# Quantised weights summed in place, their masks added in the next block

## The reference

```python
def _L0_xattn_ref(query, value, wq, wk, wv, wo):      # 32 query heads, 8 key heads, D = 128
    q = (query @ wq).reshape(b, tq, HQ, D)
    k = jnp.repeat((key @ wk).reshape(b, tk, HKV, D), REP, axis=2)
    v = jnp.repeat((key @ wv).reshape(b, tk, HKV, D), REP, axis=2)
    probs = jax.nn.softmax(jnp.einsum('bqhd,bkhd->bhqk', q * (1.0 / jnp.sqrt(D)), k), axis=-1)
    return jnp.einsum('bhqk,bkhd->bqhd', probs, v).reshape(b, tq, HQ * D) @ wo
...
    def nf4_quant_dequant(w):                          # w1, w2, w3 of layer 2, each 1376 x 512
        flat = w.reshape(-1, 64)
        absmax = jnp.max(jnp.abs(flat), axis=1, keepdims=True)
        normalized = flat / jnp.where(absmax == 0, 1.0, absmax)
        idx = jnp.searchsorted((NF4_CODE[:-1] + NF4_CODE[1:]) * 0.5, normalized)
        return (NF4_CODE[idx] * absmax).reshape(shape)
...
x = x + jnp.tanh(g_xattn[0]) * _L0_xattn_ref(_layernorm(x), ctx, ...)
x = x + jnp.tanh(g_ffn[0]) * _L0_ffn_ref(_layernorm(x), ...)   # 4-bit weights: nibbles, zero, scale
```

## Time and profile before

| | us |
|---|---|
| median of 3 runs (lowest, highest) | 1568.92 (1562.45, 1570.29) |
| the profiled execution's own time | 1567.22 |
| its span | 1565.5 |
| busy in the span: TensorE, VectorE, ScalarE, GpSimd | 1383.2, 1120.4, 677.5, 331.8 |
| the first stage's seven blocks with weights, up to VectorE's first addition of block 7 | 413.86 |

### The profile page before, as it was taken

How to read it: one execution, slowest core, us unless ns; L and a number is a source line. 1 busy time by engine, 2 the same in 40 slices (tenths; PEclk the granted TensorE clock), 3 DMA queues, 4 the chain that set the end, 5 groups by cost and what they waited for, 6 DMA issues and landing times.

```text
span 1565.5 us, 18720 instructions
## 1 busy us (share of the span) xinstructions
PE 1383.2 (88%) x6532; PEld 990.5 (63%) x6532; DVE 1120.4 (72%) x2045; ACT 677.5 (43%) x1403; POOL 331.8 (21%) x380
## 2 busy tenths in 40 slices
PE   6999999989997979987999997999999999999204
PEld 5665566556585648664788875677777777777102
DVE  4778877887887996946555555666665666667998
ACT  3777766776623443421222223444444444343104
POOL 1111111111155020221211111122122122122530
PEclk9999999999998999976999998999999999999557
DMA  5588888788820001412221310011011011000001
GB/s 210 154 203 192 180 206 202 176 182 195 191 93 1 1 27 60 85 33 68 48 68 40 112 54 14 28 41 68 27 41 68 27 41 68 1 1 1 0 0 55
DMA packets 37831, 127.76 MB, mean 82 GB/s; under 512 B 4928, under 2 KB 10944, under 8 KB 31536
## 3 DMA queue, kind: packets, MB, share of 16 engines
q1 hardware_dynamic: 26224, 83.38, 16.1%
q0 software_dynamic: 11520, 43.26, 14.5%
HBM read 72.63 MB, written 10.75 MB: 53 GB/s over the span
## 4 chain that ended last, share of the span: by engine, by line
PE 62%; DVE 20%; ACT 6%; DMA 5%; DVEq 4%; issue 2%; POOL 1%; POOLq 0%; SPq 0%
PE PS L150 11%; PE PS L152 11%; PE PS L151 11%; DMA AR<-AR 4%; DVE AR L670 4%; PE PS L913 4%; PE PS L949 4%; ACT s_sb L603 2%; DVE AR L676 2%; DVE AR L2498 2%; PE PS L935 2%; PE PS L531 2%; DVE AR L2487 2%; DVE AR L2494 2%; PE PS L506 2%
## 5 line engine op out<-in xcount | busy, mean ns | idle before, releaser
L434 POOL DMA_DIRECT2D AR<-AR x76 | 69.3, 1024 | 370.1 <-DVE AR L689 188.9
L531 PE MATMUL PS<-R,PT 128*128 128x512 f32 x256 | 122.2, 622 | 1.9 <-DVE X L710 1.8
L151 PE MATMUL PS<-R16r 128*128 128x512 f32 (+1 forms) x328 | 122.6, 374 | 0.0
L152 PE MATMUL PS<-R16r 128*128 128x512 f32 (+1 forms) x312 | 119.7, 384 | 0.0
L506 PE MATMUL PS<-R,HT 128*128 128x256 f32 x512 | 116.2, 380 | 2.3 <-ACT R L592 2.3
L506 PEld LDWEIGHTS PS<-R,HT 128*128 128x128 f32 x512 | 94.8, 190 | 14.5 <-ACT R L592 2.8
L603 ACT ACTIVATE s_sb<-PS,sm 128x64 f32<-128x64 f32 x256 | 77.9, 336 | 52.6 <-DVE sm L695 51.9
L1058 ACT COPY AR<-PS 128x512 f32<-128x512 f32 x64 | 37.5, 585 | 144.5 <-PE PS L152 144.1
L150 PE MATMUL PS<-HTr,R16r 128*128 128x512 f32 (+1 forms) x240 | 89.8, 374 | 3.0 <-DVE R16r L188 1.6
L150 PE MATMUL PS<-R16r,HTr 128*128 128x512 f32 (+1 forms) x224 | 90.2, 403 | 0.0
L531 PEld LDWEIGHTS PS<-R,PT 128*128 128x128 f32 x256 | 50.2, 200 | 60.2 <-issue 56.8
(11 more groups left out here) (311 smaller groups left out, 3590.0 us busy)
## 6 DMA issues: line engine op xcount, KB each, us to landing
AR<-AR POOLq DMA_DIRECT2D x76, 528.0 KB, 6.8
OR<-in_wo SPq DMA_DIRECT2D x12, 1024.0 KB, 4.9
dequantised<-AR SPq DMA_DIRECT2D x8, 1056.0 KB, 5.4
WR<-in_w0q SPq DMA_DIRECT2D x8, 1024.0 KB, 4.9
AR<-in_w3q SPq DMA_DIRECT2D x8, 1024.0 KB, 5.0
WR<-dequantised SPq DMA_DIRECT2D x22, 256.0 KB, 2.8
AR<-in_nf SPq DMA_DIRECT2D x4, 1056.0 KB, 6.7
nf_in<-in_nf SPq DMA_DIRECT2D x4, 1056.0 KB, 6.8
```

Of the source, the lines that this page charges most:

```text
L151: nc.tensor.matmul(out, ah, bl, start=False, stop=False)
L152: return nc.tensor.matmul(out, al, bh, start=False, stop=last_)
L434: nc.gpsimd.dma_start(nf_below(g)[:, part], what[:, part], accum_op=ALU.add, max_dma_last_dim=4 * N_NF // 2).then_inc(added, 16)
L531: i = nc.tensor.matmul(bank(5 + tt), PT[:, at:at + P], vo[:, pr, b, :], start=pr == 0, stop=pr == 1)
```

## The change

1. `up(7)` of a block writes its result into `nf_below(g)` instead of `nf_above`. All five masks, mask 0 too, go to other buffers and are added by DMA, and there is no `join`. A block has five pairs of accumulating transfers as before.
2. The masks of block g are made in block g + 1 (`masks`): two in turn 0, two in turn 1, one in turn 2. GpSimd starts the first addition after `up(7)` and mask 0.
3. `up(0)` waits for no transfer. `up(7)` of block g waits for all additions of block g - 1; mask k (k from 2) waits for the addition of mask k - 2, mask 1 for the store of the block before.
4. The steps up, the maxima and the reciprocals stand in other turns, and `far` 7, 8 and 9 earlier.
5. `load_nf` follows the last mask (turn 2, not the end of the block), `load_q` stands ahead of it, the store and the loads behind it wait for the fifth addition of a block, which now is in the next block; the load of `KR_W` waits for the last sum instead of the last addition.
6. The four norm pairs of layer 0's second norm stand between the last additions on GpSimd.

```diff
-            return nf_ring(g + 1 if k % 2 else g + 2)
+            return nf_ring(g + 1 + (k + (g == LATE)) % 2)
...
             for g in range(NG):
+                if g + 2 < NG:
+                    load_q(g + 2)
                 if g:
                     if g + 1 < NG:
                         load_nf(g + 1)
+                    if g == LATE:
+                        sp.wait_ge(A0["nf_summed"], LATE * NSUM)
+                        sp.dma_start(KR_W, l1kr_d).then_inc(A1["kr_in"], 16)
                     nf_store(sp, g - 1)
                 if g + 2 < NG:
-                    load_q(g + 2)
                     load_o(g + 2)
...
         def accumulate(pool, g, k):
-            pool.wait_ge(A0["nf_mask"], g * NDOWN + max(k + 1, 2))
-            nf_add(pool, g, k, nf_mask(g, k), "nf_left")
-            nf_add(pool, g, k, nf_mask(g, k), "nf_right")
+            if g == LATE:
+                n = k
+                pool.wait_ge(A0["nf_mask"], g * NDOWN + max(k + 1, 2))
+            else:
+                n = k + 1
+                if k == 0:
+                    pool.wait_ge(A0["nf_summed"], (g + 1) * NSUM)
+                pool.wait_ge(A0["nf_mask"], g * NDOWN + n)
+            nf_add(pool, g, n, nf_mask(g, k), "nf_left")
+            nf_add(pool, g, n, nf_mask(g, k), "nf_right")
...
             for g in range(LATE):
-                for k in range(1, NDOWN):
+                for k in range(NDOWN):
                     accumulate(pool, g, k)
-                join(pool, g)
+                    if g == LATE - 1 and k >= 2:
+                        pool_norm_pair(pool, 1, k - 2)
+            pool_norm_pair(pool, 1, PAIRS - 1)
...
-                    far(act, g, 2 * b + 1)
-                    far(act, g, 2 * b + 2)
+                    far(act, g, 2 * b + (2 if b == 3 else 1))
+                    far(act, g, 2 * b + (3 if b == 3 else 2))
...
-                if g < LATE and b == B - 1:
-                    far(act, g, NFAR)
+                if g < LATE and b == 2:
+                    far(act, g, 7)
...
             if k == 0:
-                if g:
-                    dve.wait_ge(A0["nf_left"], nf_added(g - 1, NDOWN))
-                    dve.wait_ge(A0["nf_right"], nf_added(g - 1, NDOWN))
                 nc.vector.tensor_scalar(nf_above, nf_in(g), bound, rise, ALU.is_gt, ALU.mult)\
                     .then_inc(A0["nf_summed"], 1)
             else:
+                out = nf_above
+                if k == NUP - 1 and g < LATE:
+                    out = nf_below(g)
+                    if g:
+                        dve.wait_ge(A0["nf_left"], nf_added(g - 1, NDOWN))
+                        dve.wait_ge(A0["nf_right"], nf_added(g - 1, NDOWN))
...
+            elif k == 1:
+                if g:
+                    dve.wait_ge(A0["nf_stored"], 16 * g)
+            elif k or g:
+                n = nf_added(g, k - 1) if k else nf_added(g - 1, NDOWN - 1)
                 dve.wait_ge(A0["nf_left"], n)
                 dve.wait_ge(A0["nf_right"], n)
...
+        def masks(dve, g, b):
+            for k in ((0, 1), (2, 3), (4,), ())[b]:
+                down(dve, g, k)
+            if b == 2:
+                dve.drain().then_inc(A0["nf_used"], 1)
...
                 norm(u + 1)
+                if g:
+                    masks(dve, g - 1, b)
...
             for u in range(LATE * B, NU0):
...
                 if u + 1 < NU0:
                     norm(u + 1)
+                masks(dve, LATE - 1, b)
...
-            pool_norm(pool, 1)
```

More of the change, by code:

```diff
@@ L383, in nf_store @@
             sp.wait_ge(A0["nf_right"], nf_added(g, NDOWN))
-            if g == LATE - 1:
-                sp.dma_start(KR_W, l1kr_d).then_inc(A1["kr_in"], 16)
             n = NBU * QB
@@ L427, in sp_x0, with nf_add @@
                     sp_f0(sp)
-        def nf_add(pool, g, k, what, side):
+        def nf_add(pool, g, n, what, side):
             added = A0[side]
             part = slice(0, N_NF // 2) if side == "nf_left" else slice(N_NF // 2, N_NF)
-            if g or k > 1:
-                pool.wait_ge(added, nf_added(g, k - 1))
+            if g or n > 1:
+                pool.wait_ge(added, nf_added(g, n - 1))
             nc.gpsimd.dma_start(nf_below(g)[:, part], what[:, part], accum_op=ALU.add,
@@ L679, in down @@
         def down(dve, g, k):
[L680 to L685, removed]
+            if g == LATE:
+                if k == 0:
+                    dve.drain()
+                if k == 2:
+                    dve.wait_ge(A0["nf_stored"], 16 * g)
+                else:
+                    n = nf_added(g, k - 2) if k > 2 else nf_added(g - 1, NDOWN - k)
+                    dve.wait_ge(A0["nf_left"], n)
+                    dve.wait_ge(A0["nf_right"], n)
+            elif k == 1:
+                if g:
+                    dve.wait_ge(A0["nf_stored"], 16 * g)
+            elif k or g:
+                n = nf_added(g, k - 1) if k else nf_added(g - 1, NDOWN - 1)
                 dve.wait_ge(A0["nf_left"], n)
@@ L688, in down @@
             bound, fall = DOWN[k]
-            nc.vector.tensor_scalar(nf_mask(g, k) if k else nf_below(g), nf_in(g), bound, fall, ALU.is_le, ALU.mult)\
-                .then_inc(A0["nf_mask"], 1)
+            nc.vector.tensor_scalar(nf_mask(g, k) if k or g < LATE else nf_below(g), nf_in(g), bound, fall,
+                                    ALU.is_le, ALU.mult).then_inc(A0["nf_mask"], 1)
+        def masks(dve, g, b):
[3 more added lines that the diff above has]
+                dve.drain().then_inc(A0["nf_used"], 1)
         def dve_x0(dve):
@@ L723, in dve_x0 @@
                 norm(u + 1)
+                if g:
+                    masks(dve, g - 1, b)
                 if b == 0:
-                    down(dve, g, 1)
-                    down(dve, g, 0)
-                elif b == 1:
-                    up(dve, g, 1)
-                    down(dve, g, 2)
-                elif b == 2:
-                    down(dve, g, 3)
-                    up(dve, g, 3)
-                else:
-                    up(dve, g, 5)
-                if more and b == 2:
-                    nf_reciprocal(dve, g + 1)
+                    up(dve, g, 0)
+                else:
+                    up(dve, g, 2 * b - 1 + b // 3)
+                if more and b == 3:
+                    nf_max(dve, g + 1)
                 shift(u + 2)
                 if b == 0:
-                    up(dve, g, 0)
                     lowest(dve, g, 0)
@@ L742, in dve_x0 @@
                 elif b == 1:
-                    if more:
-                        nf_max(dve, g + 1)
                     up(dve, g, 2)
@@ L747, in dve_x0 @@
                     up(dve, g, 4)
-                    down(dve, g, 4)
+                    up(dve, g, 5)
                 else:
-                    up(dve, g, 6)
+                    if more:
+                        nf_reciprocal(dve, g + 1)
                     up(dve, g, 7)
-                    dve.drain().then_inc(A0["nf_used"], 1)
-                if more and b == 3:
-                    nf_normalise(dve, g + 1)
+                    if more:
+                        nf_normalise(dve, g + 1)
             for u in range(LATE * B, NU0):
```

2 lines of the change are left out of this document (1 added, 1 removed).

## The result

The change made the kernel slower. Its median is 1588.72 us (1587.47 to 1591.59, 4 runs) against 1568.74 us (1562.45 to 1570.29, 4 runs) for the kernel before on the same chip, a ratio of 1.0138 with a 95% interval of 1.0107 to 1.0169: 20.0 us by the medians, 21.6 by the ratio. The forecast was 1555 us, faster, with a range up to 1572; both the sign and the range are wrong. The profiled execution has a span of 1584.5 us, 19 above.

What follows compares the result with a forecast made beforehand. It took TensorE as nearly full, VectorE close behind, with waits costing 6.4 us a block. Block 0 -2, blocks 1 to 5 -17, block 6 -4 and block 7 +11 gave -12: 1567.2 to 1555 us, range 1543 to 1572.

Steps and rivals of the forecast that it cites:

- The wait at `up(7)` for ScalarE goes too: VectorE's wait for ScalarE's far 9 at `up(7)` would vanish, saving 3 us a block.
- block 7's +11: Block 7, with short turns, would take 11 us more from masks, mask 3's wait and loads; between +6 and +15.
- -17 (blocks 1 to 5): Blocks 1 to 5 would each take 49.8 us instead of 53.2, 17 us less in all.
- -4 (block 6): Block 6 would take 45.8 us instead of 49.8, losing two waits and gaining mask 3's.
- L: Time of one pair of accumulating transfers, bounded by 5.9 to 11.6 us and taken as 7.3.
- quick: Rival: pairs take at most 5.5 us, no wait at mask 3, blocks of 47.0, 1535 us; chance 0.08.
- slow chain: Rival: a pair takes 9 us, mask 3 waits 7.1, blocks stay at 53.2, 1579 us; chance 0.15.
- VectorE: 46.1 + 3.7 = 49.8: Middle blocks' period in us: VectorE's own 46.1 plus a 3.7 wait at mask 3; TensorE's figure was 50.7.
- the norm pairs on GpSimd ... have slack: GpSimd's norm pairs in block 7 would come one to two additions late at worst, with slack.
- ScalarE's copy ... lands at about 48 ... 0 to 3, within the bound: Block 7: layer 1's weight load would land about 48 us after the block's first addition, costing 0 to 3 us.
- D: A block's first addition on VectorE, from which the prediction counts times within the block.
- It does nothing on TensorE: Rival: `up(0)`'s wait was already hidden, block 7's +11 stands alone, 1578 us; counted within the slow case's 0.15.

Runs made afterwards that it cites:

- experiment 1: The changed kernel with far 7 made in turn 2 ahead of the first half of the exponentials, not behind both: 1573.44 us, ratio 1.0042 to the kernel before.
- experiment 4: The kernel before with far 9 made in turn 3 ahead of the first half of the exponentials, not behind both: 1552.39 us, ratio 0.9891.
- Experiment 2: The changed kernel with layer 1's weight load issued ahead of the store of block 6 instead of behind it: 1583.43 us, ratio 1.0096 to the kernel before.
- experiment 3: The changed kernel with a buffer of its own for mask 3 of block 6: 1591.24 us, ratio 1.0151 to the kernel before.
- experiment 5: The changed kernel with three of the four norm pairs behind the last addition on GpSimd: 1587.26 us, ratio 1.0120 to the kernel before.
- experiment 11: The changed kernel with far 7 early, layer 1's weight load ahead of block 6's store and three norm pairs behind the last addition: 1566.23 us, ratio 1.0005.
- experiment 6: The changed kernel without the masks of block 6 and their additions (work left out): 1568.67 us, ratio 1.0009 to the kernel before.
- experiment 9: The kernel before with SP's load of the next block's quantised weights behind the store, far 9 unmoved: 1547.10 us, ratio 0.9868.
- after: The changed kernel, against the kernel before: 1588.72 us, ratio 1.0138.
- experiment 8: The changed kernel with far 7 early, layer 1's weight load ahead of block 6's store and an own buffer for its mask 3: 1573.35 us, ratio 1.0042.
- experiment 10: The changed kernel with far 7 early and layer 1's weight load ahead of block 6's store, no own mask buffer: 1566.32 us, ratio 0.9994.
- experiment 7: The kernel before with far 9 early and SP's load of the next quantised weights behind the store: 1534.74 us, ratio 0.9785.

## Why the prediction was wrong

**The step that failed first** is "The wait at `up(7)` for ScalarE goes too: far 9 now stands ahead of turn 3's pieces and exponentials". True of far 9, but the change pulled `up(5)` from turn 3 into turn 2, and its far 7 stands behind turn 2's exponentials. The same 3.00 us came back one turn earlier. So the term "3 us a block" for ScalarE's arrays was nothing. I had followed the step that was moved forward and not the one that took its place. Priced by experiments 1 and 4: 15 to 17 us. The second step that failed is block 7's +11, below. Term by term the prediction had -2 (block 0), -17 (blocks 1 to 5), -4 (block 6) and +11 (block 7), -12 in all; the traces have -0.4, +1.2, -2.6 and +24.6, 22.8 more at the next attention's first copy and 19 at the end.

**The additions.** L was put at 7.3. In block 3 the first pair is issued 3.98 us after the block's first addition (209.93), and mask 3's wait for the second ends at 17.24, so L = (17.24 - 3.98 - 0.2) / 2 = 6.5. Mask 3 is reached at 14.85, forecast 14.9. The wait is 2.4 instead of 3.7, so this term was a little too dear; but a second wait of 1.6 at mask 4, which I had only in a rival, makes 4.0 again. Mask 4 waits for the third pair. Its right half, issued at 223.38, has landed only by 233.7, after 10.3 us, beside the 1 MB load of query weights that SP issues at 222.54; the change had given this load a new place. Experiment 1's trace has the same (issued at 216.27 and 216.75, the mask at 226.27), but no run moved that load. By the fixed part and the rate in the Trainium skill, "DMA: Bandwidth & Descriptors", section on the anatomy of one DMA, a pair would take 4.5 us as an estimate; the trace has 6.5 in block 3. In block 7 it is 7.7, the mean of two unlike pairs: the right half of the first, beside the scales' loads and 1 MB for `KR_W` issued at 412.13, has landed by 427.08, 10.3 us after the pair's issue, and that of the second takes 5.2 (427.08 to 432.30). So neither quick nor slow chain came about.

**The block period** "VectorE: 46.1 + 3.7 = 49.8" would have been 46.1 + 2.4 + 1.6 = 50.1 without the far 7 wait; experiment 1, without it, has 50.7, TensorE's figure in the prediction. Of the -17 us for blocks 1 to 5 some 12 would have been there.

**Block 6 and block 0** gave 2.6 and 0.4 us, together 3 where I had 6.

**Block 7** was put at +11, between +6 and +15; it is +24.6. From the block's first addition to ScalarE's first copy of the next attention's probabilities it took 502.76 - 413.86 = 88.9 us before and takes 525.51 - 412.02 = 113.5. Of this 11.2 lie ahead of turn 2's addition: forecast 22 to 25 us after the first, measured 24.4, right, and right in its terms too (masks 4.8 forecast and 4.9 measured, mask 3's wait 4.7 and 4.1, loads 1.5 and 2.2). The rest comes behind it. "TensorE's chain behind them is full up to the next norm, so nothing absorbs this" was right, but the chain also grew. Turns 2 and 3, from addition to addition, take 8.4 and 9.3 us for 7.0 and 7.7: 3.0 more, with the outputs behind the 9.3 us stall at 6.67 us for 3.67 and a granted clock of 0.89 over 412 to 460, where it was 1.00 (2.4 GHz throughout) over 414 to 450 before. Then "the norm pairs on GpSimd ... have slack" and "ScalarE's copy ... lands at about 48 ... 0 to 3, within the bound" both failed. The additions are 9 us apart with a norm pair between them, so the fifth lands at D + 46.6 and not at 41; the load leaves at D + 47.3, and ScalarE's copy comes at D + 55.3 and not at 48. The transposes behind it (L264, 474.24) stand at D + 62.2, before (454.61) at D + 40.8: 21.4 more, so that 21.4 - 11.2 - 3.0 = 7.2 are left for the load and what hangs on it. Experiment 2 bears this out: the stretch is 7.3 us shorter there, and 5 to 7 us of it reach the end. The other 6 or so are those 3.0 and 3.1 more behind 474.24, where the first matmuls again run slower (1.09 us for 0.60 at L264); over the whole stretch the granted clock is 0.88, where it was 0.96. How they split between the slower clock and the norm pairs was not measured by itself: experiments 3, 5 and 11 show only that removing one wait brings up the next, and experiment 6 that without block 6's masks 20.2 of the 24.6 us go. The 4.4 that stay are not theirs; VectorE's wait of 2.5 us for the scales is among what is left.

**The rivals.** None had this outcome, and all stayed below it. "Slow chain", 1579, and "It does nothing on TensorE", 1578, came nearest, both with no gain in the blocks and a costly block 7. But the slow chain's reason didn't come about: it wants a pair of 9 us and 7.1 at mask 3, and block 3 has 6.5 and 2.39. The other's is refuted: experiments 4 and 9 show each removed wait to be worth 16 to 20 us. The waits did count; at `up(0)` the time came back at the masks, and at `up(7)` it came back at `up(5)`.

**What was aimed at.** The join's wait could be had for nothing. The prediction named the load beside the joining pair ("ran with a full load started at the same time") and used it only to price L. Experiment 9 shows that it was the cause: with the load behind the store the pair takes 7.4 us for 11.6, and is hidden.

## What to carry to other kernels

When a step is moved forward, check what it now reads and what stands in its place: a wait tied to "the step ahead of the exponentials" moves with the slot, not with the step. Before a transfer is removed, ask why it is long; here its length was the load issued beside it, and swapping two lines on SP was worth 20 us where a rewrite was worth nothing. Work deferred into the next block has to go somewhere after the last one: price that tail on every engine and queue, the loads behind the deferred store and small work on the issuing engine too.

## What the runs showed of the hardware

A pair of accumulating transfers of 528 KB a half takes 7.4 us from issue to landing with no load issued beside it (experiment 9); back to back, pairs follow each other every 6.5 us (block 3 of after). Beside a load it takes longer: 10.3 us beside the scales and 1 MB issued 4.6 us ahead of it (block 7 of after), 11.6 beside 1.1 MB issued with it (before), and 14.1 (412.98 to 427.11) beside 1.3 MB issued 2.4 us after its first half (experiment 8).

GpSimd's first computation behind its own accumulating transfers comes late. Its norm pair is two instructions with a drain between. Behind an issue the second began 8.35 us after the last issue in after (432.49 to 440.84), 8.4 in experiment 10, and 14.3 in experiment 8, where the transfer itself was drawn out by a load and landed at 427.1, 2.7 us ahead of it. So a drawn-out transfer draws out the delay. But a transfer under way isn't needed for it. Experiment 6 has no addition in block 7; its store of block 5 is issued at 408.46, so all additions had landed by then, and still its first norm pair stands 5.07 us between the two instructions:

```profile
430.73 0.22 POOL L233 TENSOR_SCALAR veps<-mv 128x2 f32<-128x2 f32 x1 [31.57 <-DVE mv L175]
436.01 0.72 POOL L235 TENSOR_TENSOR rstd<-veps,half 128x2 f32<-128x2 f32 x1 [5.07 <-issue]
```

The kernel before has 3.48 us there (427.12), with its last addition landed by 421.76, when the store leaves. The norm pairs that follow next without an issue between (459.94 in after, 430.65 in before) have 0.2 us or less there. What GpSimd waits for in these cases, and whether it is the drain, no run shows.

TensorE's clock can fall to its lower level behind a stall: in after's block 7 it is 0.89 over 412 to 460, and behind the 9.34 us stall eight matmuls took 6.67 us for 3.67. That stall cost a third more than its length. Behind the 2.57 us stall of before's block 3 eight matmuls took 4.88 us, and behind the 3.48 us stall of after's block 3 the sixteen matmuls of the scores took 3.72 us (3.62 at 215.44, with no stall ahead), with a granted clock of 1.00 over 226 to 240; so length alone doesn't tell which stall costs clock. Over 100 to 350 us the clock is 1.00 in experiments 7 and 9, where TensorE waits 2.7 and 7.6 us for ScalarE, and 0.98 in before and after, where it waits 19.4 and 22.5.
